# Two PSUM banks, one for each half, for the FP4 up products of a gated network kernel

## The reference, cut to what matters

```
def fp4_linear(x, w):
    xq = fp4_quant_dequant(x)
    wq = fp4_quant_dequant(w)
    return jnp.einsum('bsk,nk->bsn', xq, wq)
gate = fp4_linear(x, w_gate)
y = fp4_linear(x, w_up)
h = jax.nn.silu(gate) * y
return fp4_linear(h, w_down)
...
s = _L0_attn_ref(xn, ...)
g = _silu(_L0_ffn_ref(xn, L0_ffn_w_gate, L0_ffn_w_up, L0_ffn_w_down))
x = x + s * g
```

## Time and profile before

| what | us |
|---|---|
| median of 3 runs (1108.51 to 1108.95) | 1108.88 |
| the profiled execution, its own time | 1108.71 |
| its span, first to last instruction | 1107.0 |
| PE busy / PEld busy (weight loads) | 1070.9 / 967.3 |
| DVE busy | 929.2 |
| ACT busy / POOL busy | 508.1 / 50.4 |
| mean granted TensorE clock | 0.994 |

### The profile page before, as it was taken

The page is one execution under the profiler, slowest core; times in us unless marked ns, Lnnn a source line. Parts: engine busy times, 40 slices in busy tenths (PEclk is TensorE's granted clock), DMA queues, the critical chain, the costliest instruction groups (busy, mean ns, idle before and its releaser), DMA issues.

```text
span 1107.0 us, 18697 instructions
## 1 busy us (share of the span) xinstructions
PE 1070.9 (97%) x6830; PEld 967.3 (87%) x6830; DVE 929.2 (84%) x1980; ACT 508.1 (46%) x1392; POOL 50.4 (5%) x70
## 2 busy tenths in 40 slices
PE   9999999999999999999998899999999999999997
PEld 6999999999999889999987688888888888888886
DVE  6889888988889888989677888888888888888886
ACT  6654646546556465564544433333333332332322
POOL 0000000000000000000000000101010100101010
PEclk9999999999999999999999999999999999999999
DMA  7455355553554545535448222322424242333122
GB/s 242 144 166 167 114 183 159 168 172 115 179 172 147 161 149 181 168 115 166 150 146 214 76 92 81 100 91 70 127 77 133 62 133 64 114 95 115 43 74 89
DMA packets 147691, 144.40 MB, mean 130 GB/s; under 512 B 11152, under 2 KB 142608, under 8 KB 147600
## 3 DMA queue, kind: packets, MB, share of 16 engines
q1 hardware_dynamic: 147600, 143.21, 41.2%
HBM read 77.94 MB, written 65.23 MB: 129 GB/s over the span
## 4 chain that ended last, share of the span: by engine, by line
PE 69%; DVE 23%; issue 3%; DMA 2%; ACT 2%; SPq 0%; DVEq 0%
PE ps L257 50%; PE ps L667 5%; PE ps L702 4%; PE ps L708 4%; PE ps L688 4%; DVE work L1473 2%; DVE work L1491 2%; DVE r_v L1495 2%; DVE work L1468 2%; DVE work L1502 2%; DVE r_k L1429 1%; DVE work L1454 1%; DVE work L1450 1%; DVE r_v L1507 1%; DMA moved<-work 1%
## 5 line engine op out<-in xcount | busy, mean ns | idle before, releaser
L257 PE MATMUL ps<-r_k,r_gate_up 128*128 128x512 f32 x768 | 189.6, 395 | 2.7 <-DVE work L1491 2.4
L257 PEld LDWEIGHTS ps<-r_k,r_gate_up 128*128 128x128 f32 x768 | 141.0, 189 | 34.9 <-DVE work L1491 7.9
L257 PE MATMUL ps<-r_o,onT 128*128 128x256 f32 x768 | 108.0, 290 | 0.1
L257 PEld LDWEIGHTS ps<-r_q,r_v 128*128 128x128 f32 x768 | 99.4, 192 | 9.7 <-DVE r_v L1495 4.6
L257 PE MATMUL ps<-r_q,r_v 128*128 128x256 f32 x768 | 103.8, 285 | 2.0 <-DVE r_v L1495 2.0
L930 ACT ACTIVATE work<-ps 128x128 f32<-128x128 f32 x256 | 67.4, 279 | 79.9 <-PE ps L708 79.9
L1069 ACT ACTIVATE r_v<-work 128x512 fp32r<-128x512 f32 x64 | 40.5, 632 | 138.4 <-DVE work L1491 138.4
L257 PE MATMUL ps<-hT,r_k 128*128 128x512 f32 x378 | 103.2, 408 | 0.0
L257 PE MATMUL ps<-hT,r_q 128*128 128x512 f32 x384 | 98.2, 391 | 0.0
L257 PE MATMUL ps<-r_v,hT 128*128 128x512 f32 x384 | 97.4, 390 | 0.0
L257 PEld LDWEIGHTS ps<-r_o,onT 128*128 128x128 f32 x768 | 96.7, 192 | 0.3 <-DVE onT L1209 0.3
(11 more groups left out here) (151 smaller groups left out, 2025.3 us busy)
## 6 DMA issues: line engine op xcount, KB each, us to landing
moved<-work SPq DMA_DIRECT2D x63, 512.0 KB, 2.9
r_gate<-moved SPq DMA_DIRECT2D x252, 128.0 KB, 2.5
kept_h<-work SPq DMA_DIRECT2D x31, 384.0 KB, 2.6
work<-kept_h SPq DMA_DIRECT2D x124, 96.0 KB, 2.3
work<-in_L_attn_hidden_states SPq DMA_DIRECT2D x16, 512.0 KB, 5.4
kept<-work SPq DMA_DIRECT2D x9, 514.0 KB, 4.4
kept_h<-work SPq DMA_DIRECT2D x9, 512.0 KB, 3.8
work<-kept SPq DMA_DIRECT2D x8, 514.0 KB, 6.2
```

The source lines that it names most:

```text
L257: done = pe.matmul(out_ap, a, b, start=first and n == 0, stop=last and n == 2, skip_group_check=skip)
```

## The change

The two halves get a bank each. U(0) goes to bank 5 as before, and U(1) to bank 6. With two banks an up product has to wait only for the reader of its own bank, one whole chunk earlier: `h4_ready >= m - 1` in place of `h4_ready >= m`, m being the number of halves before it. The gate product keeps one bank and its wait. Ahead of block 0 the second half is issued behind the wait for the last down weights, which hold bank 6 until then.

```
+        UP4_BANKS = (B_UP4, B_TURN4)
...
                     for e in halves:
-                        m = 2 * c + e
-                        for w, bank, read, done_sem in ((wgate4, B_GATE4, s_gate4_ready, gate4_done),
-                                                        (wup4, B_UP4, h4_ready, up4_done)):
-                            if m == 0 and w is wgate4:
-                                pe.wait_ge(xT_ready, n * TURNS + KD)
-                            if n or m:
-                                pe.wait_ge(read, n * 2 * CH + m)
+                        m = n * 2 * CH + 2 * c + e
+                        for w, bank, done_sem in ((wgate4, B_GATE4, gate4_done), (wup4, UP4_BANKS[e], up4_done)):
+                            if w is wgate4:
+                                if (c, e) == (0, 0):
+                                    pe.wait_ge(xT_ready, n * TURNS + KD)
+                                if m:
+                                    pe.wait_ge(s_gate4_ready, m)
+                            elif m > 1:
+                                pe.wait_ge(h4_ready, m - 1)
...
                 pe.wait_ge(w4_ready, 2 * KD)
-                gate_up4(0, 0)
+                gate_up4(0, 0, (0,))
                 pe.wait_ge(w4_ready, 3 * KD)
+                gate_up4(0, 0, (1,))
                 pe.wait_ge(gu_ready, BLOCKS + 1)
...
-                dve.tensor_tensor(h4[:, c % 2, e * HALF4:(e + 1) * HALF4], ps[:, B_UP4, 0:HALF4],
+                dve.tensor_tensor(h4[:, c % 2, e * HALF4:(e + 1) * HALF4], ps[:, UP4_BANKS[e], 0:HALF4],
                                   s_gate4[:, e, :], ALU.mult).then_inc(h4_ready, 1)
```

## The result

| | median us (range, runs) | profiled execution, span |
|---|---|---|
| before | 1108.91 (1108.51 to 1111.26, 4) | 1108.71, 1107.0 |
| after | 1090.97 (1090.84 to 1091.24, 4) | 1091.05, 1089.3 |

The ratio is 0.9834, with a 95% interval from 0.9817 to 0.9851: 17.9 us less. The forecast was 1090.4 in a range of 1088 to 1095.

A forecast was written before the change was run, and what follows sets the result against it. TensorE and VectorE were taken to stall each other around the up products; 7 x 1.27 + 7 x 1.24 + 0.95 = 18.5 us off 1108.71 gave 1090.2, and with the median 0.17 above, 1090.4 us, range 1088 to 1095.

The forecast's parts named there:

- What bounds the kernel: Second stage: TensorE and VectorE wait for each other around the up products, two stalls a block, 15 in all.
- The price of a stall: By starts, a stall costs TensorE 1.27 us in chunk 2 and 1.24 in chunk 0; 18.5 us in all.
- The matmul row: Rival: the matmuls' own idle row gives the gain, 14.5 us, so 1094.4 us; chance 0.05.
- The first 0.95 us: Chunk 2 of the first block: its stall costs TensorE 0.95 us, which goes.
- VectorE follows: In chunks 2 and 0 P(1) moves forward by 1.28 and 1.25 us; VectorE's margin is 0.04 and 0.07 us.
- What is late next: Slice product behind P(1): about 1.4 us of margin in chunk 2, none in chunk 0, whose 0.40 us wait stays.
- Bank 6 costs nothing: Writing U(1) while VectorE reads bank 5, in 15 places: taken as no cost; 7.8 us at most.
- The order ahead of block 0: G(1) behind the wait for the last down weights: hidden, with 2.2 us to spare.
- Nothing is gained: Rival: VectorE is the bound, so the time would be 1108.9 us; chance 0.04.
- half is given back: Rival: chunk 0's seven gains return as longer slice product waits, 9.8 us left, 1099.1 us; chance 0.04.
- More is gained: Rival: waits for the slice product and its low part shrink too, by up to 9 us, to 1081; chance 0.04.
- The clock: Rival: switching banks drops TensorE's clock in each block, eight costing 25 us, 1115.7 us; chance 0.03.

The follow-up runs named there:

- e2: Changed kernel with only chunk 0's second up product freed of the wait for VectorE's first product, other chunks waiting as before; 1100.25 us, ratio 0.9912, block 59.16 us.
- e3: Changed kernel with only chunk 2's second up product freed of the wait for VectorE's first product, other chunks waiting as before; 1100.32 us, ratio 0.9905, block 59.12 us.
- e7: Changed kernel with VectorE's first slice product of each chunk one step earlier, ahead of a scaling; 1082.04 us, ratio 0.9755, block 57.03 us.
- e1: Changed kernel with its two banks, but the old wait (h4_ready >= m) restored for both up products; 1110.0 us, ratio 0.9993, block 60.40 us.
- e5: Changed kernel with an idle piece of VectorE work added ahead of P(0) in chunk 0; 1094.29 us, ratio 0.9863, block 58.52 us.
- e6: Changed kernel with an idle piece of VectorE work added ahead of P(0) in chunk 2; 1091.07 us, ratio 0.9835, block 57.87 us.
- e4: Kernel before, one bank and old wait, with VectorE doing P(0) earlier in chunks 0 and 2; 1096.23 us, ratio 0.9872, block 58.36 us.

## Why the prediction was right, point by point

*What bounds the kernel.* Right: two stalls a block on the path of both engines. e2 and e3 took them away singly, and got 1.25 and 1.29 us each.

*The price of a stall.* Right. The forecast was 1.27 in chunk 2 and 1.24 in chunk 0 and a block of 57.9; measured were 2.53 for both and 57.88. From the first block sum to the end of the span the kernel went from 1107.0 - 674.56 = 432.44 to 1089.3 - 674.58 = 414.72, by 17.72 us, against 7 x 1.27 + 7 x 1.24 = 17.6 of the working. The matmul row's 14.5 was the rival, and it is too small. That the whole time came within 0.6 us of the forecast is in part luck, since the first stage alone varies by 5 us; the block time is the real test.

*The first 0.95 us.* Right as well. In the profile after, the second stage began later (G(1) of the first block at 614.97, before at 613.20), and the block sum came at the same time: 59.61 us behind G(1), before 61.36. Of these 1.75 us a part is the clock:

```profile
614.97 1.19 PE L257 MATMUL ps<-r_gate,r_k 128*128 128x352 f32 x6 [2.75 <-ACT work L1065]
```

The same six matmuls took 2.13 us before. There the granted clock was 0.50, thus 1.2 GHz, in the window from 614 to 616; here it was 1.00 over that window, though the wait ahead was as long. In e7 they took 2.10 again. Of the eleven profiles of this study six show the slow form and five the fast one, with one bank and with two. It changes from one execution to the next, and is not the change's doing. e1, whose six matmuls also took 1.19 us, has the old wait and shows the stall by itself: from its G(1) at 613.68 to its block sum at 674.25 it took 60.57 us, 0.96 more than the changed kernel.

*VectorE follows.* Right, and the margin was thin, though not as thin as said: 0.16 us in chunk 0 in place of 0.07, by e5. The step took P(0) to hold VectorE for its whole 0.51 us and P(1) to start behind that; the next instruction that does not depend on it starts some 0.1 us sooner. For chunk 2 no number came out: e6 shows only that 0.9 us of delay there are hidden.

*What is late next.* Right for the place. The waits for the slice product stayed at 8.1 us and those for its low part at 4.6. The 0.40 us in chunk 0 is where a delay comes back (e5), and 1.4 us of slack in chunk 2 hid 0.9 (e6).

*Bank 6 costs nothing.* Right: U(1) takes 1.11 us while bank 5 is read, and the pair of products 1.04. e1 shows that it gives nothing either.

*The order ahead of block 0.* Nothing shows there; it was not tested by itself.

*The rivals.* The matmul row's 1094.4 is out of the interval of the result. "Nothing is gained" and "half is given back" fell by the block time, and in e2 and e3 each stall gave its full price. "More is gained" did not come, since the later waits count from P(1), as said. The clock stayed at 1.00 in the middle blocks. The double-buffering case of the Trainium skill's "TensorE: Matmul & The Clock Gate", section "HAM oscillation — how this bites in real kernels", where it gave nothing further, is not this one: here the product of U(1) stood on the chain, and the second bank paid off because of that.

## What to carry to other kernels

A stall in which two engines wait in turn (TensorE for the reader, then the reader for TensorE) costs both once, and both move when it goes; look whether the idle time on the other side of the wait vanishes too. Price it by the starts of instructions on either side, against the same stretch where nothing waits, and not by the idle column of the weight loads or of the matmuls. And before a second bank is spent, see why the reader is late: here moving P(0) ahead of a sum in chunk 0 and ahead of two transposes in chunk 2 gave 2.05 of the 2.53 us with a single bank.

## What the runs showed of the hardware

- The idle time of weight loads is no fixed measure of lost time: 1.25 to 1.29 us of it cost 1.24 to 1.27 ahead of a product of six 352-column matmuls (kernel before), and 0.37 cost 0.35 (e4), but 0.41 cost 0.30 and 0.26 cost 0.12 ahead of one of 512 columns (changed kernel against e7). And 0.13 us was lost in e4 where no wait row shows any.
- VectorE instructions that do not depend on one another start 0.80 us apart where the first takes 0.88 (e5), and 0.44 where it takes 0.53 (e4).
- After the same wait of 2.7 to 2.8 us TensorE went on at 1.2 GHz in some executions and at 2.4 in others: six matmuls of 352 columns in 2.13 us (before, granted clock 0.50) and 2.10 (e7), or in 1.19 (after, granted clock 1.00).
